# Recurrent steps: the next pick's column between the second and third first-layer product

## What is computed

```python
def step(h, p):
    op = jnp.argmax(h[0, 0, :NOPS])              # the pick, from the first token
    ... attention with p[...][op], taken where p['am'][op]
    z = jax.nn.relu(h @ p['w1'][op] + p['b1'][op]) @ p['w2'][op] + p['b2'][op]
    h = jnp.where(p['fm'][op], z, h)
    return (h, None)
out, _ = jax.lax.scan(step, x, xs)               # 33 steps, 19 operations
```

## Time and profile before

| | us |
|---|---|
| median of three runs | 129.36 (129.3 to 129.49) |
| span of the profiled execution, first to last instruction | 127.3 |
| recurrent part in it, first L652 to the norm's L514 | 34.25 to 47.35 |
| one step, L652 to the last L665 | 3.84 and 3.85 |

### The profile page before, as it was taken

One profiled execution on the slowest core, in us unless ns is written; L12 is line 12 of the kernel. 1 busy time (PEld: TensorE's weight loads), 2 busy tenths in 40 slices (PEclk: granted clock), 3 DMA queues, 4 the chain that ended last, 5 costly groups with the idle time before them and its releaser, 6 DMA issues.

```text
span 127.3 us, 3032 instructions
## 1 busy us (share of the span) xinstructions
PE 114.2 (90%) x1200; PEld 82.3 (65%) x1201; DVE 74.4 (58%) x149; ACT 68.3 (54%) x121; POOL 25.9 (20%) x34
## 2 busy tenths in 40 slices
PE   6989889998989899997977899999999987989990
PEld 5667566577423325877966678888888975656750
DVE  0076976718984362129999599699493004346241
ACT  4254796357630407027978959969956631347000
POOL 8996000004940000002616050050000000000000
PEclk9999999999999999999999999999999999999997
DMA  3544000000101000000000000000000000000002
GB/s 106 168 56 110 12 0 5 0 1 8 34 0 31 3 17 14 5 5 0 0 0 5 0 0 5 0 0 5 0 8 0 0 8 0 0 0 0 5 0 88
DMA packets 3060, 2.22 MB, mean 17 GB/s; under 512 B 1570, under 2 KB 2754, under 8 KB 3040
## 3 DMA queue, kind: packets, MB, share of 16 engines
q0 software_dynamic: 464, 0.67, 2.7%
q1 hardware_dynamic: 2144, 0.74, 2.4%
q10 hardware_dynamic: 432, 0.55, 1.2%
HBM read 1.68 MB, written 0.26 MB: 15 GB/s over the span
## 4 chain that ended last, share of the span: by engine, by line
PE 59%; DVE 21%; ACT 12%; issue 6%; DVEq 0%; ACTq 0%
PE ps L977 9%; PE ps L489 5%; DVE smat L913 5%; PE ps L991 5%; PE ps L1001 4%; PE ps L1293 4%; PE ps L514 3%; PE ps L496 3%; PE ps L276 3%; PE ps L287 3%; ACT tx L848 2%; DVE smatT L740 2%; PE ps L518 2%; PE ps L655 2%; ACT rstd L530 2%
## 5 line engine op out<-in xcount | busy, mean ns | idle before, releaser
L913 DVE TENSOR_TENSOR smat<-ty,tx 128x1536 f32<-128x1536 f32 (+1 forms) x14 | 21.5, 1555 | 4.3 <-ACT tx L848 4.2
L954 ACT ACTIVATE smatT<-ps 128x1536 f32<-128x1536 f32 x12 | 17.4, 1450 | 7.8 <-PE ps L977 7.6
L977 PE MATMUL ps<-cst,smat 128*128 128x128 f32 x144 | 18.1, 275 | 2.6 <-DVE smat L913 2.3
L977 PEld LDWEIGHTS ps<-cst,smat 128*128 128x128 f32 x144 | 15.7, 140 | 4.3 <-DVE smat L913 3.2
L489 PE MATMUL ps<-cst 128*128 128x256 f32 x48 | 13.0, 387 | 0.3 <-issue 0.3
L1001 PE MATMUL ps<-samp,wc 128*128 128x128 f32 x72 | 11.0, 291 | 0.0
L991 PE MATMUL ps<-smatT,xt 128*32 128x96 f32 x384 | 10.4, 249 | 0.4 <-ACT samp L945 0.4
L1001 PEld LDWEIGHTS ps<-samp,wc 128*128 128x128 f32 x72 | 8.9, 191 | 1.6
L489 PEld LDWEIGHTS ps<-cst 128*128 128x128 f32 x48 | 8.3, 190 | 2.2 <-issue 1.3
L830 POOL TENSOR_SCALAR disty<-disty 128x288 f32<-128x288 f32 x3 | 6.2, 2081 | 17.2 <-ACT disty L837 17.2
L991 PEld LDWEIGHTS ps<-smatT,xt 128*32 128x32 f32 x384 | 7.9, 109 | 2.3 <-issue 1.8
(11 more groups left out here) (200 smaller groups left out, 198.1 us busy)
## 6 DMA issues: line engine op xcount, KB each, us to landing
cst<-in_cst ACTq DMA_DIRECT2D x1, 278.0 KB, 3.5
x<-in_x SPq DMA_DIRECT2D x2, 128.0 KB, 2.9
ew<-in_L_ffn_weight POOLq DMA_DIRECT2D x4, 64.0 KB, 2.2
ew<-in_L_ffn_weight POOLq DMA_DIRECT2D x1, 256.0 KB, 4.2
w<-in_L_ffn_ffn_w SPq DMA_DIRECT2D x3, 64.0 KB
cst<-in_cst ACTq DMA_DIRECT2D x1, 129.0 KB, 3.0
out<-fin SPq DMA_DIRECT2D x1, 128.0 KB, 2.2
out<-fin ACTq DMA_DIRECT2D x1, 128.0 KB, 2.1
```

Of the source, the lines that this page charges most:

```text
L913: return nc.vector.tensor_tensor(smat[:, n % 3, BP * part.start:BP * part.stop, :].rearrange("p u (g r c) -> p (u g) r c", g=DG, c=W), ty[ ...
L954: nc.scalar.activation(smatT[:, n % 2, :, :, :].rearrange("p k g n -> p (k g n)"), ps[:, bank:bank + 3, :].rearrange("p b n -> p (b n)"), ...
L977: last = nc.tensor.transpose(ps[:, bank + u // BP, (u % BP) * P:(u % BP + 1) * P], smat[:, n % 3, u, :], ident)
```

## The change

On PE the products of groups 2 and 3 move behind the column L660 and L661, and the wait for b2 moves from ahead of L660 to ahead of L661. On DVE the pick moves ahead of the relu of group 1, so that the order is pick, relu 1, relu 3. ACT and SP are unchanged.

```diff
@@ PEBody.ffn
-                for g in range(BP):
+
+                def hidden(g):
                     rows = slice(C * g, C * g + C)
                     nc.tensor.matmul(ps[:, g, :], w1[rows, p, :], u[rows, :],
                                      start=True, stop=True).then_inc(sem("l_hid"), 1)
+
+                hidden(0)
+                hidden(1)
                 pe.wait_ge(sem("l_w2_%d" % p), 16)
-                pe.wait_ge(sem("l_b2_%d" % p), 16)
                 pe.wait_ge(sem("l_rc"), 1)
                 nc.tensor.matmul(ps[0:1, 5, 0:C], rcol[:, :], w2, start=True, stop=False)
+                pe.wait_ge(sem("l_b2_%d" % p), 16)
                 nc.tensor.matmul(ps[0:1, 5, 0:C], b2[0:C, p:p + 1], ident[0:C, 0:C],
                                  start=False, stop=True).then_inc(sem("l_col"), 1)
+                hidden(2)
+                hidden(3)
                 for g in range(BP):
                     pe.wait_ge(sem("l_relu_dve" if g % 2 else "l_relu_act"), g // 2 + 1)
@@ DVEBody.ffn
+                self.pick(dve)
                 hidden(1)
-                self.pick(dve)
                 hidden(3)
                 fetch(1 - p)
```

## The result

The changed kernel took 130.01 us (median of 20 runs, 129.47 to 130.52) against 129.38 us for the kernel before (20 runs, 128.67 to 130.24) on the same chip: a ratio of 1.005, 95% interval 1.0031 to 1.0069, or 0.40 to 0.89 us slower. All ratios leave out executions more than 1.5% above the fastest of their kernel: none of these forty, further down three of e1's ten (130.74 to 130.88), one of e2's ten (211.67) and three of 75 of the kernel before. The forecast was slower, 129.76 us with a range of 129.5 to 130.15. Sign and range were right, but the time lay nearer to rival B: one term of the sum was too small, and one that cost 0.21 stood in it at nothing.

A forecast was written before the change was run, and what follows sets the result against it. VectorE's serial work between the first-layer products and the last second-layer product was taken to bound each recurrent step. A loss of 0.20 in each of two steps, 0.40, added to 129.36 gave 129.76 us, range 129.5 to 130.15.

The forecast's parts named there:

- rival B: First step, VectorE: open small copy holds MAX8's completion until the copy ends; 0.32 more, 130.08 us; chance 0.17.
- The bound and the mechanism: Recurrent steps: VectorE's serial work bounds; its first link now waits for the column instead of product 1, losing 0.20 per step.
- (1): TensorE's column behind two products: second half at 1.455 after step start, MAX8 0.25 later at 1.705, 0.47 sooner than before.
- (2): VectorE's order pick, relu, relu: 0.87, 0.66, 0.81 bring the last L665 to 4.045 after step start, 0.20 later.
- (3): Products 2 and 3 behind the column end 2.7 to 2.95 after step start, hidden; the moved b2 wait costs nothing.
- (4): SP's loads for the next step leave 0.47 earlier, but gain nothing, as control code and fillers set the next start.
- late bound: Column on TensorE stays where it is now: loss 0.24 and 0.35 in the two steps, sum 0.59.
- C: Rival on the steps: column gets no earlier, or b2 is late; +0.59, 129.95 us; chance 0.07.
- D: Rival on TensorE: product 0 ends sooner with two products in flight; +0.20, 129.56 us; chance 0.12.
- E: Rival: the load of w1 sets the second step's start, so earlier loads pay; at most -0.27, 129.09 us; chance 0.06.

The follow-up runs named there:

- e1: Changed kernel with VectorE's order put back (relu 1, pick, relu 3), so only TensorE's order differs from the kernel before; ratio to before 0.9982.
- e2: Kernel before with only VectorE's order changed: pick ahead of both relus, TensorE as before; ratio to before 1.0049.
- e8: Kernel before with the relu of group 3 moved from VectorE to ScalarE; ratio to before 0.991.
- e9: Kernel before without the two fillers L489 that open the second step; one run, 129.44 us.
- e4: Changed kernel with VectorE's wait for w2 moved from ahead of the pick to behind it; ratio to before 1.005.
- e5: Changed kernel with the small copy to ebcol done early and without VectorE's own wait for w2; ratio to before 1.0017.
- e12: Kernel before with relu 3 on ScalarE, pick ahead of VectorE's one relu, small copy early and no fillers L489; ratio to before 0.9896.
- e7: Kernel before with one more GpSimd memset, about 1.06 us, ahead of the long one; one run, 129.57 us.
- e10: Changed kernel without the two fillers L489 that open the second step; ratio to before 1.0007.

## Why the prediction was right, and where its steps were not

**The bound and the mechanism: right.** The step is VectorE's series, and its first link now waits for the column, later than for product 1. E2 has the second step's whole loss with VectorE's half alone; e1 has none of it in its stage; and e8, which shortens the series, gains.

**(1) The column: nearly right in place, wrong in what follows it.** L665 came at T+1.42 and T+1.43 for T+1.455, and, as I had argued, not by taking products 2 and 3 out from ahead of it, since with all four ahead it comes at the same time (e2). From the start of L660 in before (T+1.35 and T+1.47) I read only that b2 was there by then, and passed over the 0.12 between them; in the second step it was the wait for b2, which e8 and e9 name in that place. The term that was mis-sized is the 0.25 from column to MAX8: it measured 0.33 (35.78 to 36.11; 43.55 to 43.87 is 0.32), because MAX8 of a step has two waits and the first pick one (e4, e5). Of 0.08 more, the column's earliness took back 0.03: 0.05 per step.

**(2) VectorE's order: right.** Pick, relu and last product took 0.88, 0.67 and 0.79 for 0.87, 0.66 and 0.81. With T+1.75 for T+1.705 the last product came at T+4.09 for T+4.045.

**(3) Products 2 and 3, and the wait for b2: right.** The relu of product 2 started on ScalarE at T+2.73 (37.09), inside my T+2.7 to T+2.95, and ended at T+3.42, ahead of the last product. b2 cost nothing, as L665 followed L663 by 0.15 in both steps. In the first step there was little room: L665 came 3.15 after the issue of b2 (32.63 to 35.78), and where L660 was held by b2 it came 3.09 (e12), 3.21 (e8) and 3.25 (e9) after it.

**(4) SP's loads: right in effect.** The second L600 left at T+3.85 instead of T+4.06; I had said 0.47 sooner; the held pick took 0.21 of that, and its two waits 0.05. It was worth nothing, as forecast: the filler L489 ends at 41.81 + 0.38 = 42.19 and L652 starts at 42.12, the overlap of the earlier trace rows, and from the last L671 to T it is 3.46 for 3.47.

**The step that failed: the argument against B, by which the hold stood in the sum at nothing.** I gave B a chance of 0.17 because the relu of before "ran beside" the open copy. That row ended at 36.51, 0.06 after the copy's 36.45, so it couldn't tell whether its end had been held; I had written down that it doesn't tell of the signal and still counted it against. With a longer memset the relu is held to the copy's end (e7). B's mechanism is real, in the first step only, and its price was 0.21 rather than 0.32 (T+4.30 against T+4.09), as MAX8 started at 36.11 where I had 35.96 (0.05 from its two waits, 0.11 from the whole step), nearer to the copy's end. By the sum alone the range would have ended at its late bound, 129.95, below what was measured; it held because I had drawn it up to B.

**The corrected sum.** 0.20 twice, 0.05 twice, and 0.21 are 0.71, and the stage shows 0.70 (13.793 against 13.096). C and D fell: the column was early, and product 0 no sooner. E fell as well: the second L652 of after waited for a filler, not w1. In before w1 was in time, by about 0.25 where e9 took the fillers away, against the 0.14 that I read. Where w1 did end last, L652 came 2.99 (e9), 3.02 (e8) and 2.80 (e12) after its issue, a spread well under the half microsecond that E needed.

**Open.** Where the rest of the span's 1.3 comes from isn't tested; its places have no part in the change. Why the clock falls in some executions with TensorE's new order isn't either. Nor was it tried to send b2 ahead of the others on SP's queue with the pick first and relu 3 on ScalarE, which e12 points to.

## What to carry to other kernels

Moving a short operation ahead in a series on the bound engine gains only if its input is there by the time the first operation now starts, and if what it releases is waited for; otherwise the engine waits at the head of the series and everything behind it moves by that wait. Look first for what can leave that engine: one relu given to a less busy neighbour was worth 0.9% here (0.6 to 1.2), and only then did the early release of the loads, and after it the order of the loads, come onto the path. And a row that ends just after a suspected blocker ends says nothing about whether it was blocked.

## What the hardware showed that I had not expected

- A VectorE operation queued behind a copy that GpSimd's memsets keep open starts, but doesn't complete before the copy: MAX8 took 0.36 and 0.95 instead of 0.17, a relu 1.61 instead of 0.75, each ending within 0.01 of the copy's end. The copy, 0.20 with GpSimd idle, stood open for 5.00.
- A second wait on VectorE's next instruction, for something already there, cost 0.07 to 0.08: column to MAX8 0.33 with two, 0.26 with one.
- In two executions with a partly idle TensorE ahead (busy 0.55 and 0.60 of a microsecond in one, 1.40 of two in the other) the granted clock fell to 0.50 soon after. In one of them it made a step 0.79 longer (6.82 against 6.03), more than the 0.51 that the missing fillers had freed (3.46 to 2.95). Over whole executions a mean of 0.987 stood in six of ten of that kernel (e10), in seven of 61 with its TensorE order and fillers, and in none of 106 with the old order and fillers.
